# A fused two-layer attention and expert kernel: one attention bias as a unit of the shared experts, another bias moved to ScalarE

## The chip, the core and the metric

The kernel runs on one core of one Trainium2 chip. The metric is device time in microseconds (us), the median of several executions. Engines are named as in the profile: PE is TensorE (matmuls; PEld its weight loads), DVE is VectorE, ACT is ScalarE, POOL is GpSimd, SP is SyncE. Matmuls write to banks of 512 fp32 columns in PSUM; everything else of this kernel lies in SBUF or in device memory.

## The reference, cut to what matters

32 sequences of 256 tokens with 128 features (8192 tokens) go through two layers. Each layer is `x = x + attention(norm(x)) + experts(norm(x))`. Of the biases only two are touched:

```python
# layer 0: linear attention, 16 heads, and 8 routed experts (top 2) plus shared ones
out = einsum('bse,fe->bsf', out, Wo) + bo                     # bo: output bias
shared = silu(xf @ swg) * (xf @ swu) @ swd                    # 352 hidden units
# layer 1: causal attention, 8 heads, with a gate u
u = silu(x @ Wu.T + bu)                                       # bu: bias of units
out = (u * rms_norm(out, scale)) @ Wo.T + bo
```

All biases hold random values, so none can be left out.

## The kernel before, in words

The program is written out by hand for each engine; an engine runs its instructions in the order written, and semaphores are the only link between engines. Tokens are handled in 16 groups of 512 (four tiles of 128), `NG` = 16. Four stages follow one another:

1. **Attention 0** (about 0 to 255 us), steps 2 to 19. Step s works on group g = s - 2 (queries, keys and values, shared experts' hidden units) and on group e = s - 3 (its state, mixing and `output0`). Beside it LayerNorm, routing on DVE, and on POOL the sending of each routed row to its expert's region in device memory: 256 indirect DMAs, spread over the steps by the table `SENDS`, each behind a matmul of its step (`behind_attention0`). When all have landed, SP loads the first tile of rows of the experts; the last step's PE work (`rows_to_columns(0, 0, 3)`) waits for it, and `output0(15)` stands behind that on PE.
2. **Experts 0** (about 255 to 420 us): 36 tiles, bound by PE.
3. **Attention 1** (about 420 to 668 us), steps 2 to 20, same grouping: for group g keys, values and units, for group e = g - 1 energies and their use with the values, for y = g - 2 the output. DVE also adds the experts' rows of layer 0 (L1507), takes LayerNorm statistics and routes for layer 1.
4. **Experts 1** (about 668 to 936 us).

The lines that matter here:

- A product is exact to nearly fp32 by being split in high and low parts. A bias is likewise split in two rows (high and low) of the tile `bias` (`biases`, L1308 to L1311), and added by a matmul with ones: `bias_by_token` (L655) puts it along the tokens, `bias_by_feature` (L659) along the features. L655 is called in `keys_values0` (twice per group), in `output0` (once per group) and in attention 1's `v_of`; L659 in `u_of` alone.
- `output0(e)` adds into bank 7 the bias, then the attention's product (L748, 8 matmul instructions), then the shared experts' down product (L754, 24 instructions), whose hidden units `sh_h` come from DVE in three chunks of 128 (L1384). 352 units are used; the last 32 rows of the third chunk are zero padding.
- `constants_once` on DVE stands in the opening between LayerNorm statistics of groups 2 and 3 and before the split of the first weights (L1329) and columns (L1338), for which the first product of attention 0 (L674) waits.
- Attention 1, per group, around the change: PE `u_of` (bias L659, product L976, fp32 in four passes) into bank 1; ACT `tanh1` (L1888) of half the sum; DVE `units1` (L1561): (tanh + 1) * sum, read from bank 1. ACT then goes on with `keys_by_token` (L1894), `normalise` (L1673, rows of the LayerNorm, in the steps that have one), `heads1` (L1881) and `columns` (L1678). PE transposes these rows (L614), does the output (L1039, behind DVE's state L1565) and the next queries (L939). `keys_by_token` of PE (L981) also waits for the totals (ACT L1912) and, in steps with logits, for their copy (ACT L1691).
- POOL masks half of the energies with an affine select (L2109) that reads and writes SBUF, once per half step.

## Time and profile before

| | us |
|---|---|
| three runs | 933.10, 934.08, 941.79 |
| median | 934.08 |
| the profiled execution's own time | 937.29 |
| its span, first to last instruction | 935.8 |
| PE busy | 845.9 (90%) |
| DVE busy | 694.5 (74%) |
| ACT busy | 575.4 (61%) |
| POOL busy | 627.7 (67%) |

The mean granted TensorE clock is 0.975 of full. The busy shares are means over four stages with different limits: PE is 90% busy in the whole, yet in the attention stages it shares the chain of waits with DVE, ACT and POOL. So a change inside one stage is to be read in that stage: in the chain of waits there, and in the order of time around the line.

### The profile page before, as it was taken

Reading aid. Unit: us, or ns where it says so; the run is one execution under the profiler, and the core shown is the slowest. Engines: PE = TensorE matmul, PEld = TensorE weight load, DVE = VectorE, ACT = ScalarE, POOL = GpSimd, SP = SyncE. Lnnn points to the kernel's source line nnn. Section 1 sums busy time; section 2 is a strip of 40 time slices with the busy share of each in tenths; the row PEclk is TensorE's granted clock in tenths of the full one; section 3 lists DMA queues with packets and bytes.
Section 4 is the critical chain, followed back from the end, with each engine's and each line's share of the span. In section 5 each row is a group of like instructions: output and inputs, shape, how many; then the busy total and the mean of one; then the engine's idle time right before and its main releaser. Section 6 shows DMA issues by size and latency. Waiting matters only on the chain.

```text
span 935.8 us, 22379 instructions
## 1 busy us (share of the span) xinstructions
PE 845.9 (90%) x7975; PEld 752.8 (80%) x7975; DVE 694.5 (74%) x1809; ACT 575.4 (61%) x1185; POOL 627.7 (67%) x607
## 2 busy tenths in 40 slices
PE   3789999999699999997898888887899899999997
PEld 3678888889699998984566666665798899999996
DVE  7777787886377998885788788878654465668776
ACT  5756555454366777668886776654565375756652
POOL 4157677777105888876788788866777777666663
PEclk9999999999899999998999999989899899999999
DMA  9799992117449998951111111113776687789996
GB/s 269 233 407 397 395 385 67 48 52 236 166 144 286 311 302 263 289 163 54 37 39 41 35 36 43 42 34 112 278 237 200 214 283 258 255 296 344 363 365 184
DMA packets 130990, 191.06 MB, mean 204 GB/s; under 512 B 15808, under 2 KB 85952, under 8 KB 130752
## 3 DMA queue, kind: packets, MB, share of 16 engines
q1 hardware_dynamic: 96720, 141.21, 44.8%
q0 software_dynamic: 16640, 34.37, 11.1%
q10 hardware_dynamic: 17520, 14.06, 4.8%
q8 instruction: 64, 1.05, 0.5%
q14 instruction: 46, 0.38, 0.1%
HBM read 110.74 MB, written 80.97 MB: 205 GB/s over the span
## 4 chain that ended last, share of the span: by engine, by line
PE 58%; DVE 22%; issue 6%; ACT 5%; SPq 4%; DMA 3%; POOL 3%; DVEq 0%; POOLq 0%; ACTq 0%
PE pair L887 13%; PE pair L834 5%; PE pair L835 5%; PE pair L833 5%; PE pair L864 3%; PE pair L754 3%; PE pair L667 3%; PE pair L1031 2%; DVE a_en L1574 2%; PE pair L1008 2%; DVE X L1507 2%; ACT a_rows L1673 2%; DVE stats_t L1142 2%; PE pair L674 2%; PE pair L676 1%
## 5 line engine op out<-in xcount | busy, mean ns | idle before, releaser
L1992 POOL DMA_INDIRECT sent<-a_rows,slot x224 | 221.2, 987 | 84.3 <-issue 55.5
L2094 POOL DMA_INDIRECT back<-ex_tile_out,address x136 | 150.2, 1105 | 60.4 <-issue 31.1
L2003 POOL DMA_INDIRECT ex_joined<-outs,slot x128 | 132.1, 1032 | 86.6 <-DMA outs<-ex_tile_out 50.3
L833 PE MATMUL pair<-ex_x_hi,ex_w_hi 128*128 128x256 f32 x497 | 148.0, 298 | 0.0
L834 PE MATMUL pair<-ex_x_lo,ex_w_hi 128*128 128x256 f32 x497 | 142.1, 286 | 0.0
L835 PE MATMUL pair<-ex_x_hi,ex_w_lo 128*128 128x256 f32 x497 | 142.0, 286 | 0.0
L887 PE MATMUL pair<-ex_stage,ex_hid 128*128 128x128 f32 x1136 | 132.5, 275 | 0.0
L887 PEld LDWEIGHTS pair<-ex_stage,ex_hid 128*128 128x128 f32 x1136 | 130.0, 192 | 0.0
L1708 ACT ACTIVATE ex_w_hi<-ex_stage 128x768 fp32r<-128x768 f32 (+1 forms) x72 | 67.5, 937 | 91.6 <-DMA ex_stage<-in_experts 91.5
L1834 ACT ACTIVATE ex_hid<-pair,ex_stage 128x256 f32<-128x256 f32 x284 | 107.1, 497 | 0.1
L1345 DVE TENSOR_TENSOR ex_w_lo<-ex_stage,ex_w_hi 128x768 fp32r<-128x768 f32 (+1 forms) x72 | 77.4, 1075 | 31.6 <-ACT ex_w_hi L1708 30.8
L834 PEld LDWEIGHTS pair<-ex_x_lo,ex_w_hi 128*128 128x128 f32 x497 | 96.3, 194 | 0.0
L835 PEld LDWEIGHTS pair<-ex_x_hi,ex_w_lo 128*128 128x128 f32 x497 | 96.1, 193 | 0.0
L833 PEld LDWEIGHTS pair<-ex_x_hi,ex_w_hi 128*128 128x128 f32 x497 | 96.1, 193 | 0.0
L1986 POOL TENSOR_TENSOR rstd<-variance,minus_half 128x4 f32<-128x4 f32 x32 | 41.0, 1281 | 49.0 <-DVE variance L1147 48.5
L864 PE MATMUL pair<-ex_stage,ex_hid 128*128 128x128 f32 x568 | 69.7, 276 | 2.0 <-DVE ex_hid L1464 2.0
L864 PEld LDWEIGHTS pair<-ex_stage,ex_hid 128*128 128x128 f32 x568 | 66.5, 192 | 3.3 <-issue 3.2
L1673 ACT ACTIVATE a_rows<-X,shift,rstd 128x128 f32<-128x128 f32 x112 | 45.7, 486 | 30.2 <-DVE shift L1152 30.2
L1351 DVE TENSOR_TENSOR ex_x_lo<-pair,ex_x_hi 128x512 fp32r<-128x512 f32 x72 | 49.0, 680 | 15.3 <-ACT ex_x_hi L1714 14.6
L1824 ACT ACTIVATE ex_gate_s<-pair 128x512 f32<-128x512 f32 (+1 forms) x72 | 42.1, 587 | 27.4 <-PE pair L835 22.1
L674 PE MATMUL pair<-a_xT_hi,a_w_hi 128*128 128x512 f32 x112 | 49.5, 442 | 6.2 <-DVE a_xT_lo L1338 5.3
L1464 DVE TENSOR_TENSOR ex_hid<-ex_gate_s,pair 128x512 f32<-128x512 f32 (+1 forms) x72 | 48.9, 679 | 7.8 <-ACT ex_gate_s L1824 5.7
(247 smaller groups left out, 1992.7 us busy)
## 6 DMA issues: line engine op xcount, KB each, us to landing
ex_stage<-in_experts SPq DMA_DIRECT2D x72, 578.0 KB, 5.3
outs<-v_heads SPq DMA_DIRECT2D x8, 4352.0 KB
ex_stage<-in_experts SPq DMA_DIRECT2D x72, 320.0 KB, 4.2
ex_tile_in<-sent SPq DMA_DIRECT2D x72, 128.0 KB
outs<-ex_tile_out SPq DMA_DIRECT2D x71, 128.0 KB
ex_joined<-back ACTq DMA_DIRECT2D x15, 512.0 KB, 8.1
ex_tile_in<-sent SPq DMA_DIRECT2D x54, 132.0 KB
X<-in_x SPq DMA_DIRECT2D x16, 256.0 KB, 5.2
```

Source lines behind the costliest of these rows:

```text
L674: pe.matmul(o, w0_hi[:, c:c + P], hi, start=True, stop=False)
L833: pe.matmul(o[:, of_half], wh, x_hi[i % 2][:, of_half], start=True, stop=False)
L834: pe.matmul(o[:, of_half], wh, x_lo[i % 2][:, of_half], start=False, stop=False)
L835: m = pe.matmul(o[:, of_half], wl, x_hi[i % 2][:, of_half], start=False, stop=True)
L864: m = pe.matmul(bank[7][:, i * C:(i + 1) * C], hid[n % 2][c][:, i * P:(i + 1) * P], stage[0][n % NSTAGE[0]][:, i // HALF, 2 * F0P + c * C: ...
L887: m = pe.matmul(bank[b][:, s * C:(s + 1) * C], hid[n % 2][c][:, s * P:(s + 1) * P], stage[1][n % NSTAGE[1]][:, s // HALF, F1 + c * C:F1 + ...
L1345: dve.tensor_tensor(w_lo[layer][n % NSTAGE[layer]][:, 0:k, 0:u], stage[layer][n % NSTAGE[layer]][:, 0:k, 0:u], w_hi[i % 2][:, 0:k, 0:u].bi ...
L1708: act.activation(w_hi[i % 2][:, 0:k, 0:u], stage[layer][n % NSTAGE[layer]][:, 0:k, 0:u], ACT.Copy).then_inc(w_hi_here, 1)
L1834: m = act.activation(hid[n % 2][c][:, of_half], bank[c][:, of_half], ACT.Gelu, bias=stage[1][n % NSTAGE[1]][:, h, b1:b1 + 1])
L1992: pool.indirect_dma_start(out=sent[layer], out_offset=bass.IndirectOffsetOnAxis(ap=slot_i[layer][k][:, s, j:j + 1], axis=0), in_=rows[laye ...
L2003: pool.indirect_dma_start(out=joined[g % NJOIN][:, j, k, :], out_offset=None, in_=outs, in_offset=bass.IndirectOffsetOnAxis(ap=slot_i[0][k ...
L2094: pool.indirect_dma_start(out=back, out_offset=bass.IndirectOffsetOnAxis(ap=address[i % NSIDE][:, s // HALF, s % HALF:s % HALF + 1], axis= ...
```

## The change

Three things are edited.

- **bo of layer 0.** The matmul with ones in `output0` goes; the first product L748 starts the bank (`start=(i == 0)`). Row 96 of the third chunk of hidden units, until now padding, is set to 2.0 once by DVE, and the same row of the down weights (halved on the chip like the rest) holds bo. The second op of `shared_hidden` writes only the first 96 rows of the third chunk.
- **bu of layer 1.** The matmul L659 goes. `tanh1` gets half of bu as a per-partition bias. A new ACT instruction, `units1`, writes bank 1 plus bu to the SBUF tile `u1`, after ACT's `keys_by_token` and before `normalise`; it waits for results of layer 0 (at g = 1) and for `uo_ready`. DVE's `units1` takes its second operand from `u1` in SBUF and waits for `u1_here` too. PE's next users of bank 1 (`k_of`, the transposes) wait for `u1_here` in place of `u1_ready`.
- **Housekeeping.** `bias` has three blocks for five; `cols` has a fifth column; `constants_once` makes `half_bu` and four memsets; the loads of x of groups 8 to 15 share a semaphore by pairs.

```diff
@@ constants_once (DVE)
+                dve.tensor_scalar(half_bu[:], cols[:, 4:5], 0.5, None, ALU.mult)
+                for i in range(2):
+                    own(dve.memset(sh_h[i][2][SHARED_REST:P, :], 0.0))
+                    dve.memset(sh_h[i][2][SHARED_REST:SHARED_REST + 1, :], 2.0)
-                biases(0, 3 * C).then_inc(consts_made, 1)
+                biases(0, 2 * C).then_inc(consts_made, 1)
@@ next_layer_once (DVE)
-                biases(3 * C, 5 * C).then_inc(consts1_made, 1)
+                biases(2 * C, 3 * C).then_inc(consts1_made, 1)
@@ output0 (PE)
-                bias_by_token(7, 2 * C, C)
                 pe.wait_ge(mix0_ready, e + 1)
...
-                                  start=False, stop=False, skip_group_check=True)
+                                  start=(i == 0), stop=False, skip_group_check=True)
@@ shared_hidden (DVE)
+                k = SHARED_REST if c == 2 else P
-                dve.tensor_tensor(sh_h[g % 2][c][:], s, bank[3 + (2 * c + 1) % 3], ALU.mult).then_inc(sh_ready, 1)
+                dve.tensor_tensor(sh_h[g % 2][c][0:k, :], s[0:k, :], bank[3 + (2 * c + 1) % 3][0:k, :], ALU.mult).then_inc(sh_ready, 1)
@@ k_of, and the transposes of attention 1 (PE)
-                    pe.wait_ge(u1_ready, g)
+                    pe.wait_ge(u1_here, g)
@@ u_of (PE)
-                bias_by_feature(1, 4 * C)
-                pe.matmul(bank[1], w_attn1[:, 3 * C:4 * C], flat(xTg(g)), start=False, stop=True).then_inc(u1_done, 1)
+                pe.matmul(bank[1], w_attn1[:, 3 * C:4 * C], flat(xTg(g)), start=True, stop=True).then_inc(u1_done, 1)
@@ units1 (DVE)
                 dve.wait_ge(u1_tanh, g + 1)
-                if g == 1:
-                    results_back(dve, NTILES - 1)
-                dve.scalar_tensor_tensor(u1[g % 2][:], th1[1][:], 1.0, bank[1], ALU.add, ALU.mult).then_inc(u1_ready, 1)
+                dve.wait_ge(u1_here, g + 1)
+                dve.scalar_tensor_tensor(u1[g % 2][:], th1[1][:], 1.0, u1[g % 2][:], ALU.add, ALU.mult).then_inc(u1_ready, 1)
@@ ACT: a new function, and its place in the step
+            def units1(g):
+                act.wait_ge(u1_done, g + 1)
+                if g == 1:
+                    results_back(act, NTILES - 1)
+                if g >= 2:
+                    act.wait_ge(uo_ready, g - 1)
+                act.activation(u1[g % 2][:], bank[1], ACT.Identity, bias=cols[:, 4:5]).then_inc(u1_here, 1)
...
-                act.activation(th[:], bank[b], ACT.Tanh, scale=0.5).then_inc(said, 1)
+                act.activation(th[:], bank[b], ACT.Tanh, bias=bias, scale=0.5).then_inc(said, 1)
...
-                    tanh1(u1_done, g, 1, th1[1], u1_ready, u1_tanh)
+                    tanh1(u1_done, g, 1, th1[1], u1_ready, u1_tanh, half_bu[:])
                     keys_by_token(g)
+                    units1(g)
@@ host
+    swd[2 * P + SHARED_REST] = i["L0_attn_bo"]
```

## Rows read from the trace of the kernel before

**Rows 1.** The page, chain that ended last: share of the span by engine.

```profile
PE 58%; DVE 22%; issue 6%; ACT 5%; SPq 4%; DMA 3%; POOL 3%; DVEq 0%; POOLq 0%; ACTq 0%
```

**Rows 2.** Chain of waits, attention 0: start us, us, what.

```profile
64.50 0.24 PE pair L655
...
197.68 0.24 PE pair L655
```

**Rows 3.** Order of time on POOL: start, us, engine, line, op, tiles [idle before].

```profile
203.35 0.96 POOL L1992 DMA_INDIRECT sent<-a_rows,slot  x1 [0.72 <-PE pair L676]
204.73 0.96 POOL L1992 DMA_INDIRECT sent<-a_rows,slot  x1 [0.42 <-PE pair L676]
...
237.85 0.96 POOL L1992 DMA_INDIRECT sent<-a_rows,slot  x1 [0.31 <-issue]
```

**Rows 4.** Chain of waits, end of attention 0.

```profile
237.85 3.67 DMA sent<-a_rows,slot
...
246.78 0.43 PE pair L655
```

**Rows 5.** Order of time, all engines, opening.

```profile
1.20 0.22 DVE L1298 MEMSET scan<- 128x192 f32 x1
...
1.94 0.57 DVE L1303 MEMSET before<- 128x272 f32 x2
...
16.56 0.77 PE L674 MATMUL pair<-a_xT_hi,a_w_hi 128*128 128x512 f32 x1 [3.79 <-DVE a_xT_lo L1338]
```

**Rows 6.** Order of time, all engines, one step of attention 1.

```profile
483.17 0.48 PE L659 MATMUL pair<-ones_r,bias 128*128 128x512 f32 x1
...
484.08 0.21 ACT L1691 ACTIVATE logit<-pair 128x32 f32<-128x32 f32 x1
...
484.36 0.20 PEld L981 LDWEIGHTS pair<-consts,a_k 128*128 128x128 f32 x2 [0.68 <-ACT rms L1912]
...
484.55 0.60 ACT L1888 ACTIVATE a_th<-pair 128x512 f32<-128x512 f32 x1 [0.25 <-PE pair L976]
485.04 0.38 ACT L1894 ACTIVATE a_ktok<-pair 128x256 f32<-128x256 f32 x1
485.17 0.69 DVE L1561 SCALAR_TENSOR_TENSOR a_u<-a_th,pair 128x512 f32<-128x512 f32 x1 [0.78 <-ACT a_th L1888]
...
486.94 0.42 DVE L1565 TENSOR_TENSOR a_kv<-pair,consts 128x256 f32<-128x256 f32 x1 [1.07 <-PE pair L988]
```

**Rows 7.** Chain of waits, attention 1: steps where ACT or DVE decides.

```profile
427.15 3.07 ACT a_rows L1673 x8
...
561.68 0.59 DVE a_u L1561
```

**Rows 8.** Instructions on tile bias: duration ns min/median/max, first and last start, forms.

```profile
L1308 DVE CAST bias<-a_bias_raw x2: 294/320/345, 10.6 to 223.6; 128x384 fp32r<-128x384 f32 x1, 128x256 fp32r<-128x256 f32 x1
L1309 DVE TENSOR_TENSOR a_bias_raw<-a_bias_raw,bias x2: 427/493/559, 11.0 to 224.0; 128x384 f32<-128x384 f32 x1, 128x256 f32<-128x256 f32 x1
L1311 DVE SCALAR_TENSOR_TENSOR bias<-bias,consts,a_bias_raw x2: 485/552/618, 12.0 to 224.9; 128x384 fp32r<-128x384 f32 x1, 128x256 fp32r<-128x256 f32 x1
```

**Rows 9.** Order of time on ACT: instructions with a bias per partition.

```profile
486.84 1.51 ACT L1881 ACTIVATE a_kh<-a_k,consts 128x512 f32<-128x512 f32 x2
...
489.51 0.69 ACT L1814 ACTIVATE a_e<-pair,bqk1neg 128x512 f32<-128x512 f32 x1 [0.67 <-PE pair L939]
```

**Rows 10.** Order of time, DVE and POOL, three places in attention 1.

```profile
487.28 2.47 DVE L1507 SCALAR_TENSOR_TENSOR X<-ex_joined,gates_tok,X 128x128 f32<-128x128 f32 x8
...
500.54 1.10 POOL L2109 TENSOR_SCALAR_AFFINE_SELECT a_en<-a_en 128x1024 f32<-128x1024 f32 x1
500.57 3.32 DVE L1507 SCALAR_TENSOR_TENSOR X<-ex_joined,gates_tok,X 128x128 f32<-128x128 f32 x8
...
561.30 1.10 POOL L2109 TENSOR_SCALAR_AFFINE_SELECT a_en<-a_en 128x1024 f32<-128x1024 f32 x1
```

**Rows 11.** Stretch: length, busy us (instructions) of each engine, clock, DMA share, GB/s.

```profile
428.00:441.50 13.50, 10.17 (x104) 6.50 (x105) 8.15 (x25) 10.07 (x19) 8.87 (x9) 0.75 0.11 36
```

More of the change, by code:

```diff
@@ L52 @@
 SPLIT0 = 3 * C + 2 * FSP
+SHARED_REST = 352 - 2 * P
 WO0, SD0 = SPLIT0, SPLIT0 + C
@@ L249, in build @@
         gates = sb("gates", [P, 2, NARROW])
-        cols = sb("cols", [P, 4])
+        cols = sb("cols", [P, 5])
+        half_bu = sb("half_bu", [P, 1])
         bo1 = sb("bo1", [P, C])
@@ L258, in build @@
         bqk1neg = sb("bqk1neg", [P, 2])
-        bias = sb("bias", [P, 5 * C], F32R)
+        bias = sb("bias", [P, 3 * C], F32R)
         ones_r = sb("ones_r", [P, 512], F32R)
@@ L338, in build @@
         pads = a0("pads", [P, E, HALF, ROW])
-        bias_raw = a0("bias_raw", [P, 5 * C])
+        bias_raw = a0("bias_raw", [P, 3 * C])
         pad_addresses = a0("pad_addresses", [P, NPAD, HALF])
@@ L401, in build @@
         bank = [pair[i // 2][:, 512 * (i % 2):512 * (i % 2 + 1)] for i in range(8)]
-        x_dma = [sem(f"x_dma{g}") for g in range(NG)]
+        x_dma = [sem(f"x_dma{g}") for g in range(8 + (NG - 8) // 2)]
+        x_sem, x_count = [*range(8), *(8 + g // 2 for g in range(NG - 8))], [16] * 8 + [32] * (NG - 8)
         const_dma, small_dma, out_dma = sem("const_dma"), sem("small_dma"), sem("out_dma")
@@ L656, in bias_by_token @@
                           start=True, stop=False, skip_group_check=True)
-            def bias_by_feature(b, a):
-                pe.matmul(bank[b], bias[:, a:a + C], ones_r[:], start=True, stop=False)
             def rows_to_columns(layer, n, b):
@@ L967, in v_of @@
                 pe.wait_ge(q1_max, g + 1)
-                bias_by_token(0, 3 * C, C)
+                bias_by_token(0, 2 * C, C)
                 for i in range(GT):
@@ L1096, in tensor_program @@
                 for k, n in enumerate(COLUMNS[1].get(step, ())):
-                    pe.wait_ge(u1_ready, g + 1)
+                    pe.wait_ge(u1_here, g + 1)
                     if k == 1:
@@ L1137, in statistics @@
                 if layer == 0:
-                    dve.wait_ge(x_dma[g], 16)
+                    dve.wait_ge(x_dma[x_sem[g]], x_count[g])
                 else:
@@ L1882, in heads1, with tanh1 @@
                 m.then_inc(kh1_ready, 1)
-            def tanh1(done, g, b, th, ready, said):
+            def units1(g):
[5 more added lines that the diff above has]
+                act.activation(u1[g % 2][:], bank[1], ACT.Identity, bias=cols[:, 4:5]).then_inc(u1_here, 1)
+            def tanh1(done, g, b, th, ready, said, bias=0.0):
                 act.wait_ge(done, g + 1)
@@ L2189 @@
     swd = padded_rows(i["L0_ffn_swd"], 3 * P)
-    bias = np.concatenate([i[f"L0_attn_b{n}"] for n in "kvo"] + [i[f"L1_attn_b{n}"] for n in "vu"])[None, :]
+    swd[2 * P + SHARED_REST] = i["L0_attn_bo"]
+    bias = np.concatenate([i["L0_attn_bk"], i["L0_attn_bv"], i["L1_attn_bv"]])[None, :]
     arrays = {
```

6 lines of the change are left out of this document (3 added, 3 removed).

## The prediction

> **What bounds the kernel now.** I read the page's chain of waits first, then the chain in order of time through the two attention stages, then the order of time of each engine around the edited lines, and last the stretches with their granted clock. The page's chain is 58% PE, but 22% DVE and 5% ACT [rows 1], so a matmul that goes is worth something only where PE ends last. The experts' stages (some 430 us) hold nothing that is edited; they only start earlier or later.
>
> In attention 0 the chain runs through PE from the third bias matmul of a step on (L655 before L748 and L754) in seven steps up to 198 us; the first and the last of them stand in [rows 2], at 0.24 us each. In the others, among them the one from 178 to 193 us, it runs through ACT and DVE. From 203 us on POOL decides: its sends follow each other every 1.26 us (0.96 and a gap of 0.30) from 204.73 to 237.85 without a longer gap [rows 3]; they last waited for PE at 203.35 and 204.73, with gaps of 0.72 and 0.42. Then the last send lands, a tile is loaded, and PE does the last `output0` on the chain, bias at 0.43 us because the clock is at half [rows 4].
>
> In the opening, DVE ends last: the first product stands 3.79 us idle until DVE's split of columns [rows 5], and `constants_once` lies in DVE's queue ahead of it.
>
> In attention 1 a step takes 12 to 17 us. Steps are named here by their group g. PE's L659 is followed by L976 and L981. L981's weights are loaded at 484.36, straight after ACT's copy of the logits (484.08 + 0.21), not after L976 [rows 6]. DVE waits 0.78 us for the tanh before L1561, and 1.07 us for PE before L1565. The chain passes through ACT's normalised rows in g = 0 (427.15) and g = 1, and through DVE's L1561 in g = 3, 9, 10, 11, 13 and 14, of which the one of g = 9 stands in [rows 7].
>
> **The opening.** Four memsets of 512 columns are added. The nearest rows are 0.22 us for 192 columns and 0.57 for two of 272 [rows 5]: 0.285 each, or 0.065 more for 80 columns, which gives 0.22 + 320 x 0.0008 = 0.48 for 512. Four are 1.9 us, less a small overlap: 1.75. `half_bu` is one small instruction, 0.1. The biases shrink from 384 to 256 columns, which the two forms show directly: 0.05 + 0.13 + 0.13 us [rows 8], and about 0.1 for L1310 between them, 0.4 in all. Net 1.4 us, all of it on the path: DVE has no gap there. Bounds: 0.3 (memsets as short as the 0.22 row, 4 x 0.22 - 0.4 - 0.2 of overlap) and 2.1 (0.57 each, nothing of it overlapped). I take +1.4, by the slope. `biases` for layer 1 also shrinks, at 224 us, where POOL decides: nothing. Loads of x by pairs: groups 8 and 9 are first used 48 us in, when the loads have long landed: nothing.
>
> **Attention 0.** 16 matmuls go. Seven of them at 0.235 are on the chain before POOL takes over: 1.65 us. POOL can follow: it had 0.42 + 0.12 us of slack at 203.35 and 204.73 beyond its 0.30 gap [rows 3], and only one or two steps' savings (0.235 each) have to come out of it, as it waits for PE at the start of nearly every step before. The savings behind 203 us are lost, because the 27 sends left take 34 us whatever PE does. The last bias, 0.43 us at half clock [rows 4], is on the chain again. Together -2.1 us; bounds 0.43 (POOL keeps its times) and 16 x 0.235 + 0.2 = 4.0. DVE's op with 96 for 128 rows costs the same, as its length is set by columns. The down product has no more instructions than before.
>
> **Attention 1, the matmul.** L659 costs PE 0.24 us between starts, 16 times. But L981 cannot follow it: it is held by ACT's logits or totals [rows 6], which hang on the energies before L659. In g = 2 to 14 that leaves at most 0.03 us a step, 0.15 in all. Only in g = 15, without such a wait, the whole 0.24 comes through.
>
> **Attention 1, the new ACT instruction.** With a bias per partition an ACT op of 512 columns from PSUM takes 0.69 us (L1814) against 0.60 without (L1888) [rows 6, 9]. What counts is the distance between starts: 0.49 from L1888 to L1894 [rows 6], and 0.75 for each of the pair L1881 with two such operands [rows 9]; for one I take the middle, 0.62. So tanh + 0.13, copy + 0.62, and, where the tanh was waiting for PE, 0.24 earlier: `normalise` starts 0.51 later. In g = 0 the tanh waits for ACT itself, so 0.75. These two steps have ACT's rows on the chain [rows 7]: +1.26 us. In g = 2 to 8 the rows and so L614, L1039, L939 come 0.5 later too, but DVE is the one that ends the step there, with about 1 us to spare between the last use of values and DVE's gated units; nothing, and if that cover were gone, 0.5 each. Queued behind the copy on ACT are the rows, heads and columns; behind them PE's transposes.
>
> **Attention 1, DVE.** L1561 now waits for the copy: 0.35 + 0.38 = 0.73 us later than before where it waited for the tanh. In most steps the 1.07 us before L1565 [rows 6] take that up. Not in g = 10, where routing follows directly; it is counted below.
>
> There is a second cost, in the operands. Before, L1561 read one SBUF tile and PSUM; now it reads two SBUF tiles. Eight DVE ops with several SBUF inputs take 2.47 us beside DMA work of POOL, and 3.32 when they start inside an affine select (L2109): the DVE is held until the select has ended [rows 10]. L1561 itself started inside such selects in 11 of 16 steps, unhurt. From now on it would be held until about 0.54 us after the select's end (0.69 less the 0.15 of fixed time already spent). At g = 9 the select runs from 561.30 to 562.40 and L1561 started at 561.60 [rows 7, 10]: end at 562.94 for 562.28, +0.66, straight on the chain. By the same working g = 11 loses 0.6, g = 10 0.6 (with the wait above; its scan was being held already), g = 3 0.3 (PE was late there too), g = 13 and 14 under 0.05, and in g = 1, 2, 8 and 12 it ends before L1565 is due. Sum +2.2 us; bounds 0 and 16 x 0.6.
>
> The Trainium skill says of this, in "SBUF — State Buffer", section "Who interferes with whom", that a VectorE instruction with two SBUF inputs contends with a GpSimd instruction that reads SBUF, and that the one that starts first blocks the other. The trace agrees for the select (2.47 against 3.32), and by the page alone one would also fear the 7 steps in which VectorE comes first and the select is held for 0.69 us; the trace has no chain through the select there.
>
> **Sum.** 1.4 - 2.1 - 0.4 + 1.3 + 2.2 = +2.4 us. Against the profiled execution's own time of 937.29 that is 939.7. That execution lies 3.2 above the median of the three runs, 934.08; carried over, 936.5.
>
> **Rivals.**
>
> *PE is the bound wherever it loses a matmul* (faster). Then 32 matmuls at 0.235 go, 7.5 us, and the copies hide in ACT's idle time (39% of the span): 934.1 - 7.5 - 0.2 + 1.4 = 927.8. For it: PE at 90%. Against it: L981's wait, POOL from 203 us on. Chance 0.10.
>
> *The gains as forecast, the additions hidden* (about equal or a little faster). DVE's two-input op is not held because semaphores move it past the select, and the opening's memsets overlap: -2.1 - 0.4 + 0.3 + 0.5 = -1.7, 932.4. Chance 0.22.
>
> *The copy sits in every step* (slower). Place: ACT between `keys_by_token` and `normalise`, or `heads1` in steps without rows, with the transposes and the next queries behind it. It decides if the time from the rows to DVE's gated units shrinks by more than about 1 us in a step. Price: 16 x 0.62 = 9.9 for 1.3 + 2.2, so 934.1 + 1.4 - 2.1 - 0.4 + 9.9 = 942.9. For it: g = 0 and 1 are bound so now. Against it: DVE is without a gap before its gated units in g = 2 and 4 to 8. Chance 0.10.
>
> *The clock* (slower). In 428 to 441.5 the granted clock is 0.75 of full on average [rows 11], after PE had waited for ACT's rows; there half of the stretch ran at 1.2 GHz. A longer wait for rows could bring such a stretch to other steps. Price: 13.5 us with half of it at half speed lost about 3 us against its neighbours. Two more of them would give 936.5 + 6 = 942.5. Chance 0.06.
>
> *The matmuls go but time doesn't follow at all*, since the moved bias rides in products that run anyway: this is not in doubt, the instruction counts are plain.
>
> **Numbers.** The forecast has 0.52. Its own range is 934 to 939.5. The predicted time is 936.5. The range for 8 in 10 goes to the hidden-additions case and its lower bound of attention 0, 930.5, and up to just under the two slow rivals, 942. A measurement of this kernel tells about 1% (9.3 us) from no change: faster by more would need under 924.7, which no case reaches by its own sum (0.03, for the runs' own spread of 8 us); slower by more needs above 943.4, the upper edge of the two slow rivals (0.06).
>
> **What would show it.** First product at 18.0 in place of 16.56. No gap over 0.31 on POOL from about 204 on, and its last send some 0.2 us earlier than 237.85 (opening against savings). The gap before L981's weights still ended by ACT. `normalise` of g = 0 and 1 later by 0.75 and 0.5 behind the tanh. L1561 taking 1.0 to 1.5 us where it starts inside L2109. The attention 1 stage 3.1 us longer, and both experts' stages the same. It would be wrong if L1561 keeps 0.69 us in every step, if the first product keeps its 16.6, or if the span of attention 1 changes by over 5 us.

## The result, and the profile after

| | median us | runs | ratio to before |
|---|---|---|---|
| before, beside the change | 937.69 (933.10 to 943.92) | 15 | 1 |
| changed | 943.79 (938.65 to 950.05) | 15 | 1.0058 [1.0037, 1.0079] |
| before, in the third set of runs | 1033.25 | 35 | 1 |
| changed, in the third set of runs | 1036.07 | 12 | 1.0026 [0.9995, 1.0058] |

In the third set the kernel before too takes 1033 us, in another condition of the chip, and only the ratio is to be compared. The ratio on record, with its 95% interval, is not the quotient of the two medians: that is 1.0065 in the first measurement, or 6.1 us. By the ratios the change makes the kernel slower: 5.4 us (3.5 to 7.4) in the first measurement, 2.7 (-0.5 to 6.0) in the second, whose interval includes no change. The forecast was +2.4 and 936.5 us, in a range from 930.5 to 942.0. The direction held; the size and the range did not. Half of the 7.3 us from 936.5 to 943.79 is the kernel before itself: its 15 runs (the first three among them) have a median of 937.69, 3.6 above the 934.08 of the three to which the forecast was carried over. The rest, 5.4 us by the ratio against 2.4, is the subject here.

The profiled execution of the changed kernel took 938.86 us, span 937.4, against a span of 935.8 before. So the two traces differ by 1.6 us, not by 5.4: the profiled execution is the second fastest of the changed kernel's 15. What the traces show is therefore read stage by stage, against the spread that a stage has where nothing was edited.

The page of the changed kernel, first the busy time, then the chain that ended last:

```profile
PE 838.7 (89%) x7943; PEld 743.2 (79%) x7943; DVE 698.6 (75%) x1814; ACT 586.5 (63%) x1201; POOL 635.2 (68%) x607
...
PE 51%; DVE 23%; issue 7%; ACT 5%; POOL 5%; SPq 5%; DMA 3%; DVEq 0%; ACTq 0%; POOLq 0%
```

PE has 32 instructions fewer and is 7.2 us less busy, yet its share of the chain fell from 58 to 51% and POOL's rose from 3 to 5 [rows 1]. The chain moved to other engines by far more than 7.2 us. Part of this is a near tie that fell the other way: before, the chain goes through PE until 231.5 us, although POOL's gaps are no longer than 0.31 us from 204.73 us on [rows 3], and in the changed kernel it goes through POOL's sends from 206 us on. So the shares of the chain are no prices.

**Opening.** In order of time, the changed kernel on DVE and PE:

```profile
11.16 0.48 DVE L1326 MEMSET a_sh_h<- 32x512 f32 x1
11.81 0.48 DVE L1327 MEMSET a_sh_h<- 1x512 f32 x1 [0.17 <-DVE a_sh_h L1326]
12.35 0.48 DVE L1326 MEMSET a_sh_h<- 32x512 f32 x1
13.00 0.48 DVE L1327 MEMSET a_sh_h<- 1x512 f32 x1 [0.17 <-DVE a_sh_h L1326]
13.50 0.29 DVE L1307 CAST bias<-a_bias_raw 128x256 fp32r<-128x256 f32 x1
...
19.09 0.77 PE L675 MATMUL pair<-a_xT_hi,a_w_hi 128*128 128x512 f32 x1 [6.03 <-DVE a_xT_lo L1343]
```

Each memset has the 0.48 us of the estimate, but they occupy DVE from 11.16 to 13.50, 2.34 us: the second of a pair must wait for the first (0.17), and starts of independent ones are 0.54 apart (11.81 to 12.35), which is more than 0.48. PE's idle time before the first product grows from 3.79 [rows 5] to 6.03, and the product starts 2.53 us later. The rows of DVE account for all of it: 2.34 for the memsets, 0.28 from the start of `half_bu` to that of the first memset, less 0.38 for the shorter biases (1.58 us in place of 1.96), is 2.24; the other 0.29 are the landing of the first input, for which DVE waits until 5.72 us in place of 5.43 and which no edit touches.

**Attention 0.** On POOL, and then the chain of waits at the end of the stage:

```profile
204.68 0.96 POOL L2008 DMA_INDIRECT sent<-a_rows,slot  x1 [0.46 <-PE pair L677]
206.06 0.96 POOL L2008 DMA_INDIRECT sent<-a_rows,slot  x1 [0.42 <-PE pair L677]
...
239.40 0.95 POOL L2008 DMA_INDIRECT sent<-a_rows,slot  x1 [0.31 <-issue]
```

```profile
239.40 2.92 DMA sent<-a_rows,slot
...
246.51 1.09 PE pair L668 x4
247.60 1.71 PE pair L748 x8
249.31 2.96 PE pair L754 x24
```

As in [rows 3], POOL waits for PE up to 206 us and then runs at its own pace. DVE's first operation on the queries of a group stands 2.92 us later than before in g = 1, 2.40 in g = 7, 1.56 in g = 11 and 1.33 in g = 13; POOL's last send is 1.54 later. So of the 2.53 us of the opening 1.0 was won back before POOL decided; g = 14 and 15 fall to 1.06 and 0.79, which reaches nobody. On the last chain the products L748 follow the columns L668 without a bias between them [rows 4]. Experts 0 begins at 252.45 for 252.27: 2.53 lost, 2.35 won, at the first product of the experts.

**Attention 1.** The step of g = 9, in order of time, all engines:

```profile
562.88 0.17 ACT L1927 ACTIVATE rms<-pair 128x4 f32<-128x4 f32 x1
...
563.16 0.69 ACT L1903 ACTIVATE a_th<-pair,half_bu 128x512 f32<-128x512 f32 x1
563.20 0.20 PEld L980 LDWEIGHTS pair<-consts,a_k 128*128 128x128 f32 x2 [0.91 <-ACT rms L1927]
...
563.74 0.38 ACT L1909 ACTIVATE a_ktok<-pair 128x256 f32<-128x256 f32 x1
564.01 0.69 ACT L1897 ACTIVATE a_u<-pair,cols 128x512 f32<-128x512 f32 x1
...
564.50 1.10 POOL L2125 TENSOR_SCALAR_AFFINE_SELECT a_en<-a_en 128x1024 f32<-128x1024 f32 x1
564.58 1.64 ACT L1679 ACTIVATE a_rows<-X,shift,rstd 128x128 f32<-128x128 f32 x4
564.80 1.35 DVE L1567 SCALAR_TENSOR_TENSOR a_u<-a_th,a_u 128x512 f32<-128x512 f32 x1
...
565.56 1.48 POOL L2130 TENSOR_TENSOR rms<-rms,plus_half 128x4 f32<-128x4 f32 x1
```

The same step before, DVE's units and POOL's next instruction:

```profile
561.60 0.68 DVE L1561 SCALAR_TENSOR_TENSOR a_u<-a_th,pair 128x512 f32<-128x512 f32 x1
...
562.37 1.08 POOL L2114 TENSOR_TENSOR rms<-rms,plus_half 128x4 f32<-128x4 f32 x1
```

Line L980 (L981 before) has the same wait as in [rows 6], 0.91 for 0.68 us, ended by ACT (0.68 in g = 9 before, too): the matmul that went only lengthened the wait. DVE's units operation starts inside the affine select and takes 1.35 us in place of 0.69; it ends at 566.15, 0.55 after the select. POOL pays as well: its small TENSOR_TENSOR behind the select starts while DVE's held operation runs and takes 1.48 us for 1.08, ending 0.90 after DVE's. This is so in 10 of the 16 steps (1.48 to 1.53 us, for at most 1.16 before), and POOL is busy 635.2 us for 627.7. The forecast has no such term, and no run here shows what it costs in time. All 16 of DVE's operations by form, and the step of g = 4 in order of time:

```profile
L1897 ACT ACTIVATE a_u<-pair,cols x16: 688/690/692, 426.9 to 651.5; 128x512 f32<-128x512 f32 x16
L1567 DVE SCALAR_TENSOR_TENSOR a_u<-a_th,a_u x16: 691/700/2096, 427.7 to 652.3; 128x512 f32<-128x512 f32 x16
```

```profile
489.66 2.10 DVE L1567 SCALAR_TENSOR_TENSOR a_u<-a_th,a_u 128x512 f32<-128x512 f32 x1 [1.57 <-ACT a_u L1897]
490.10 1.10 POOL L2125 TENSOR_SCALAR_AFFINE_SELECT a_en<-a_en 128x1024 f32<-128x1024 f32 x1
```

Here DVE's row starts first, by 0.44 us, and DVE was held all the same, until 0.56 us after the select's end; the select kept its 1.10. The traces with the bu part alone and with the memsets at the top show the same step with 2.12 and 2.11 us. The Trainium skill says in "SBUF — State Buffer", section "Who interferes with whom", that the order of issue decides which of the two blocks the other. By the starts of the rows that did not hold in this step; but a row doesn't show when its instruction was issued, so the rule is neither confirmed nor refuted here. In g = 0 and 1 ACT's copy and rows are on the chain, and then the clock is low. Chain of waits of the changed kernel, answering to [rows 7]:

```profile
427.04 0.58 ACT a_u L1897
427.62 3.06 ACT a_rows L1679 x8
...
443.55 0.58 ACT a_u L1897
444.12 3.07 ACT a_rows L1679 x8
```

Two stretches of the changed kernel, g = 0 and g = 1, and the same two steps before (length, busy us and instructions of PE, PEld, DVE, ACT and POOL, granted clock, DMA share, GB/s):

```profile
421.90:436.70 14.80, 10.58 (x29) 5.66 (x29) 7.04 (x24) 10.85 (x22) 9.22 (x10) 0.57 0.14 47
436.70:454.30 17.60, 14.32 (x179) 9.50 (x179) 10.36 (x28) 13.28 (x25) 9.45 (x10) 0.79 0.09 28
```

```profile
422.80:436.20 13.40, 8.30 (x30) 4.44 (x30) 7.07 (x24) 10.23 (x22) 9.38 (x10) 0.80 0.16 52
436.20:451.80 15.60, 12.73 (x181) 8.95 (x180) 10.37 (x27) 12.60 (x24) 9.41 (x10) 0.96 0.10 32
```

The clock granted in g = 0 is 0.57 for 0.80 and in g = 1 0.79 for 0.96. That the change of this stage did it is not shown: the kernel with the bo part alone, whose attention 1 is the kernel before's, has clocks nearly as low and steps as long (14.4 and 17.5 us from query to query):

```profile
425.00:440.00 15.00, 10.07 (x34) 5.23 (x38) 7.57 (x24) 10.44 (x23) 8.75 (x9) 0.69 0.15 49
440.00:457.00 17.00, 14.12 (x179) 9.66 (x179) 9.92 (x28) 12.42 (x24) 9.48 (x10) 0.80 0.08 26
```

What a low clock costs stands in PE's products behind the rows of g = 1, first changed, then before:

```profile
449.71 2.04 PE L939 MATMUL pair<-xT,w_attn 128*128 128x512 f32 x2 [1.63 <-ACT xT L1684]
451.68 1.94 PE L1030 MATMUL pair<-a_en,v_heads 128*32 128x128 f32 x32
```

```profile
449.05 1.10 PE L939 MATMUL pair<-xT,w_attn 128*128 128x512 f32 x2 [1.74 <-ACT xT L1678]
450.07 1.08 PE L1031 MATMUL pair<-a_en,v_heads 128*32 128x128 f32 x32
```

The wait before them is as long as before (1.63 and 1.74), and the same instructions take 0.9 us more each at the lower of the two levels, 1.2 GHz.

### The profile page after: what moved, and what is told of

Its sections match the earlier page's. It is cut to its first block, busy times and chain, and to the rows that moved or that the text cites. A ratio compares the mean times of both kernels' runs of the same rounds, so it can differ in the third digit from the quotient of the medians.

```text
span 937.4 us, 22382 instructions
## 1 busy us (share of the span) xinstructions
PE 838.7 (89%) x7943; PEld 743.2 (79%) x7943; DVE 698.6 (75%) x1814; ACT 586.5 (63%) x1201; POOL 635.2 (68%) x607
## 4 chain that ended last, share of the span: by engine, by line
PE 51%; DVE 23%; issue 7%; ACT 5%; POOL 5%; SPq 5%; DMA 3%; DVEq 0%; ACTq 0%; POOLq 0%
PE pair L887 12%; PE pair L833 4%; PE pair L834 4%; PE pair L835 4%; POOL sent L2008 3%; PE pair L864 3%; PE pair L754 2%; PE pair L668 2%; DVE a_en L1580 2%; PE pair L1030 2%; PE pair L1007 2%; ACT a_rows L1679 2%; DVE stats_t L1141 2%; DVE X L1514 2%; SPq L558 2%
## 5 line engine op out<-in xcount | busy, mean ns | idle before, releaser
L2019 POOL DMA_INDIRECT ex_joined<-outs,slot x128 | 134.4, 1050 | 83.7 <-PE pair L668 47.4
L2110 POOL DMA_INDIRECT back<-ex_tile_out,address x136 | 152.2, 1119 | 55.9 <-issue 31.1
L833 PE MATMUL pair<-ex_x_hi,ex_w_hi 128*128 128x256 f32 x497 | 146.4, 295 | 0.0
L833 PEld LDWEIGHTS pair<-ex_x_hi,ex_w_hi 128*128 128x128 f32 x497 | 94.8, 191 | 0.0
L2002 POOL TENSOR_TENSOR rstd<-variance,minus_half 128x4 f32<-128x4 f32 x32 | 39.1, 1222 | 51.0 <-DVE variance L1146 50.6
L1486 DVE TENSOR_TENSOR ex_tile_out<-pair,ex_b2o 128x512 f32<-128x512 f32 (+1 forms) x37 | 24.8, 670 | 44.1 <-PE pair L887 43.8
```

What stands on the lines that cost most here:

```text
L833: pe.matmul(o[:, of_half], wh, x_hi[i % 2][:, of_half], start=True, stop=False)
L2019: pool.indirect_dma_start(out=joined[g % NJOIN][:, j, k, :], out_offset=None, in_=outs, in_offset=bass.IndirectOffsetOnAxis(ap=slot_i[0][k ...
L2110: pool.indirect_dma_start(out=back, out_offset=bass.IndirectOffsetOnAxis(ap=address[i % NSIDE][:, s // HALF, s % HALF:s % HALF + 1], axis= ...
```

## The experiments

Twelve measurements of eleven kernels, in three sets; a set shares a chip and 35 runs of the kernel before, and each of the twelve has 12 runs. In the second and third set the kernel before takes 1033 us. The instructions last nearly as long as elsewhere (L833 has a mean of 295 to 298 ns in the changed kernel), but its chain shows 5% of "another core or an unknown queue", some 50 of the 95 us, and DVE stands idle for 23 to 24 us somewhere between 738 and 772 us in all eight traces of this condition and in none of the first. The first set, at 938 us, and the second, at 1033, name the same chip. No run here tells what the cause is. So ratios and stages are compared only within one condition.

| kernel | ratio | interval |
|---|---|---|
| set 1: bo part alone | 1.0004 | 0.9976 to 1.0031 |
| bu part alone | 1.0027 | 1.0001 to 1.0053 |
| bo part, memsets at the top | 0.9982 | 0.9959 to 1.0005 |
| whole change, memsets at the top | 1.0021 | 0.9987 to 1.0055 |
| set 2: copy stays in PSUM | 1.0013 | 0.9992 to 1.0034 |
| no copy | 0.9992 | 0.9978 to 1.0006 |
| whole change, more matmuls in g = 0, 1 | 1.0006 | 0.9986 to 1.0026 |
| bo part at the top, more matmuls in g = 0, 1 | 0.9966 | 0.9939 to 0.9993 |
| set 3: whole change | 1.0026 | 0.9995 to 1.0058 |
| whole change, more matmuls in g = 0, 1 | 1.0001 | 0.9973 to 1.0028 |
| before, more matmuls in g = 0, 1 | 0.9989 | 0.9960 to 1.0018 |
| before without the 32 matmuls | 0.9981 | 0.9950 to 1.0013 |

The stages of the profiled executions, in us, worked out from the starts of these events: the first product, POOL's last send of attention 0, the first product of each expert stage, and DVE's first operation on the queries in g = 0 and g = 2 of attention 1; the last stage ends with DVE's last instruction.

| kernel | first product | to last send | to experts 0 | experts 0 | att. 1, g = 0, 1 | att. 1, rest | experts 1 |
|---|---|---|---|---|---|---|---|
| before | 16.56 | 221.3 | 14.4 | 170.6 | 29.0 | 217.5 | 264.1 |
| changed | 19.09 | 220.3 | 13.1 | 169.4 | 32.4 | 218.4 | 262.3 |
| bo alone | 18.77 | 220.1 | 13.6 | 172.6 | 31.9 | 215.8 | 265.0 |
| bu alone | 17.00 | 221.2 | 14.8 | 171.6 | 30.2 | 218.7 | 263.9 |
| bo, top | 16.19 | 220.1 | 13.4 | 173.1 | 30.0 | 217.4 | 264.5 |
| changed, top | 16.55 | 219.6 | 14.6 | 171.0 | 32.4 | 218.3 | 262.9 |
| *before, more matmuls* | 16.46 | 245.1 | 13.8 | 190.5 | 30.2 | 236.6 | 291.8 |
| *without the 32* | 16.45 | 243.0 | 12.9 | 191.1 | 31.4 | 236.2 | 295.1 |
| *changed, again* | 18.79 | 245.0 | 12.6 | 191.0 | 33.1 | 237.4 | 293.2 |
| *copy in PSUM* | 18.81 | 245.3 | 12.5 | 191.8 | 32.8 | 236.5 | 291.1 |
| *no copy* | 18.68 | 243.9 | 12.6 | 193.9 | 30.6 | 234.5 | 296.8 |
| *changed, more m.* | 18.67 | 243.7 | 12.4 | 189.1 | 30.2 | 238.1 | 293.7 |
| *changed, more m., again* | 18.97 | 244.7 | 13.5 | 190.9 | 30.2 | 238.3 | 295.5 |
| *bo, top, more m.* | 16.16 | 243.5 | 13.0 | 191.2 | 29.0 | 235.3 | 294.8 |

(In italics the second condition.) The expert stages carry none of the edits, and vary by 3.7 and 2.6 us in the first condition alone. A single trace can't be trusted for a sum; the attention stages are averaged over several kernels with the same part. The ratios have the same weakness: by its medians (937.18 against 937.79) the whole change with the memsets at the top would be 0.6 us faster than before, by its ratio 2.0 slower.

**The bo part alone, and with its memsets at the top.** Output bias as a unit, second attention as before:

```diff
 # bo alone: as in the change, bu's matmul, tanh and units as before
 # memsets at the top: the same four as the first instructions of DVE
+            for i in range(2):
+                own(dve.memset(sh_h[i][2][SHARED_REST:P, :], 0.0))
+                dve.memset(sh_h[i][2][SHARED_REST:SHARED_REST + 1, :], 2.0)
             dve.memset(ones_bf[:], 1.0)
```

> The kernel before with the part of layer 0 alone: bo as a unit of the shared experts, with the memsets where the change has them. Theory A (the cost is additive and lies in two places: 2.5 us in the opening, 4 to 5 us in attention 1, less 1.7 to 2.2 us in attention 0): the first product starts at about 19.1 us, attention 0 wins 1.7 us of that back before POOL takes over, the experts of layer 0 start within 0.4 us of before, attention 1 keeps its steps; in all 0 to +0.5 us against before. Theory B (PE is the bound and the matmuls were worth 0.235 us each): attention 0 wins 3.8 us, in all -1.3 us. Theory C (the loss is this part's, by the opening carried to the end): +2.5 us or more.

> The part of layer 0 alone, but its four memsets stand first in DVE's program, where DVE waits about 3 us for the first x. Theory A: the first product starts at 16.1 to 16.6 us (the biases are shorter by 0.4), attention 0 wins 1.7 to 2.2 us and nothing gives it back: -2.0 to -2.6 us against before, faster than before by 0.2 to 0.3%. Theory B: -4.2 us. Theory C': POOL's sends from 203 us on decide alone and keep their times: 0.

The opening in order of time, memsets at the top:

```profile
0.97 0.48 DVE L1297 MEMSET a_sh_h<- 32x512 f32 x1 [0.97 <-PEq L2211]
1.62 0.48 DVE L1298 MEMSET a_sh_h<- 1x512 f32 x1 [0.17 <-DVE a_sh_h L1297]
2.17 0.48 DVE L1297 MEMSET a_sh_h<- 32x512 f32 x1
2.82 0.48 DVE L1298 MEMSET a_sh_h<- 1x512 f32 x1 [0.17 <-DVE a_sh_h L1297]
...
16.19 0.76 PE L675 MATMUL pair<-a_xT_hi,a_w_hi 128*128 128x512 f32 x1 [3.54 <-DVE a_xT_lo L1341]
```

The same memsets cost nothing where DVE waits for input anyway: the first product is at 16.19, earlier than before by the shorter biases. With the memsets in place it is at 18.77. The difference is 2.58 us, of which 0.14 are the landing of the first input (5.47 for 5.33), so the place costs about 2.4. It is carried on: the experts of layer 0 begin at 249.74 us with the memsets at the top, 252.44 with them in place and 252.27 before. The ratios point the same way (1.0004 in place, 0.9982 at the top), but their intervals overlap and each includes 1. By the ratio the bo part without its opening is worth -1.7 us (-3.8 to +0.5); attention 0 was forecast at -2.1. Theory C of the part in place (+2.5 us) is at the edge of the ratio's interval (+2.9), and it is the trace that speaks against it.

**The bu part alone.** The change with the bo edits undone:

```diff
+                bias_by_token(7, 2 * C, C)
                 pe.wait_ge(mix0_ready, e + 1)
...
-                                  start=(i == 0), stop=False, skip_group_check=True)
+                                  start=False, stop=False, skip_group_check=True)
```

> The kernel before with the part of layer 1 alone: no matmul L659, the bias copy on ACT, the semaphores of x by pairs. Theory A: the opening and attention 0 as before; attention 1 from its first queries to the first tile of the experts after it 4 to 5 us longer: about 1.5 and 2 in g = 0 and 1, 0.6 to 1.0 in each of g = 3, 4, 9, 10, 11 where DVE's units op is held by POOL's select; in all +4 to +5 us. Theory B (PE bound): -3.8 us. Theory C (the loss is the opening's): 0.

Its ratio, 1.0027, is +2.5 us (+0.1 to +5.0); attention 1 is 248.9 us long for 246.5. That is near the prediction's terms for attention 1 (-0.4 + 1.3 + 2.2 = +3.1), and less than the 4 to 5 us expected for this run, which had been taken from the changed kernel's trace. Theory B (-3.8 us) is excluded.

**The whole change with the memsets at the top.** The edit is the one above, on the changed kernel.

> The whole change, the four memsets first in DVE's program. Theory A: 2.2 to 2.6 us less than the changed kernel, so +2.5 to +3.5 us against before; the first product at 16.2 to 16.8 us. Theory B and C: if the opening's loss is absorbed anyway, the same as the changed kernel.

1.0021 where the changed kernel has 1.0058: the first product comes 2.5 us earlier by the trace (16.55), and the ratios differ by 3.5 us with overlapping intervals. The expectation of +2.5 to +3.5 us against before was a little high for a ratio of +2.0.

**The copy left in PSUM.** Now DVE's units read one SBUF tile and PSUM, as before the change, while ACT does the same additional instruction:

```diff
-                act.activation(u1[g % 2][:], bank[1], ACT.Identity, bias=cols[:, 4:5]).then_inc(u1_here, 1)
+                act.activation(bank[1], bank[1], ACT.Identity, bias=cols[:, 4:5]).then_inc(u1_here, 1)
...
-                dve.scalar_tensor_tensor(u1[g % 2][:], th1[1][:], 1.0, u1[g % 2][:], ALU.add, ALU.mult).then_inc(u1_ready, 1)
+                dve.scalar_tensor_tensor(u1[g % 2][:], th1[1][:], 1.0, bank[1], ALU.add, ALU.mult).then_inc(u1_ready, 1)
```

PE's two users of bank 1 wait for `u1_ready` again.

> The whole change, but ACT's copy adds bu in place in PSUM bank 1; DVE's units op then reads one SBUF tile and PSUM as before, and PE waits for DVE's op before it reuses the bank. Theory A1 (DVE's op with two SBUF inputs is held by POOL's select, and that is half of the loss in attention 1): the op takes 0.69 us in all 16 steps, steps g = 3, 4, 9, 10, 11 are 0.5 to 1 us shorter than in the changed kernel, 2.5 to 3 us in all; g = 0 and 1 unchanged. Theory A2 (the copy's time on ACT is the whole loss): no step but those bound by ACT changes, and attention 1 stays at the changed kernel's length.

By form, and where the operation starts inside a select (g = 3):

```profile
L1567 DVE SCALAR_TENSOR_TENSOR a_u<-a_th,pair x16: 676/687/689, 474.8 to 711.2; 128x512 f32<-128x512 f32 x16
```

```profile
524.44 1.10 POOL L2125 TENSOR_SCALAR_AFFINE_SELECT a_en<-a_en 128x1024 f32<-128x1024 f32 x1
524.79 0.68 DVE L1567 SCALAR_TENSOR_TENSOR a_u<-a_th,pair 128x512 f32<-128x512 f32 x1
```

The longest of the 16 takes 0.69 us, though the operation stands as late as with the copy to SBUF and starts inside a select in 10 of the 16 steps. With the copy in SBUF it takes up to 1.31 us in this condition and 2.12 in the first. POOL's TENSOR_TENSOR behind the select is back at 1.04 to 1.07 us too. That settles what holds them: the second SBUF operand. In time it gives 1.3 us (1.0013 for 1.0026 in the third set), which the intervals can't tell from nothing; the rest of attention 1 is 236.5 us long for a mean of 237.9 of the three traces with the copy in SBUF. The 2.5 to 3 us that theory A1 expected were not found: the mechanism is shown, its price is not.

**No copy at all.** DVE reads bank 1 directly, bu only enters the tanh; this leaves the bias out of the linear factor of the units.

```diff
                     keys_by_token(g)
-                    units1(g)
...
-                dve.wait_ge(u1_here, g + 1)
```

> The whole change without ACT's copy: bu is left out of the linear factor of the units and stays only in the tanh; DVE reads bank 1 as before. Theory A: attention 1 within 1 us of the kernel before (only 0.1 us per tanh is left in g = 0 and 1), so 3.5 to 4.5 us less than the changed kernel, and in all +0 to +1 us against before (opening +2.5, attention 0 -2.3). Theory B (losing the matmuls shifts PE's clock stretches, the copy is harmless): attention 1 stays 3 us or more longer than before.

0.9992, 3.5 us less than the changed kernel (1.0026): the additional ACT instruction and the held operation together. The sum had 1.3 + 2.2 for the two. It is a difference of two sets with overlapping intervals, though, and the agreement may be partly luck: from g = 2 on this kernel's attention 1 is 234.5 us long, 1.7 to 2.1 shorter than in the two kernels of this condition whose DVE operation is the same as here (236.2 and 236.6).

**More matmuls in g = 0 and g = 1.** Four products of 512 columns in each of the two steps, into a bank that nobody reads, while PE waits for the rows: one ahead of the transposes, one behind the first set and two behind the second. The waits for the readers of that bank are left out below. They were put into the changed kernel, the kernel with the bo part at the top and, in the third set, the kernel before.

```diff
+                if warm:
+                    pe.matmul(bank[4], w_attn1[:, 0:C], flat(xTg(0)), start=True, stop=True)
                 for k, n in enumerate(COLUMNS[1].get(step, ())):
...
                     transposes(1, n, 1 - k)
+                    if warm:
+                        for _ in range(k + 1):
+                            pe.matmul(bank[4], w_attn1[:, 0:C], flat(xTg(0)), start=True, stop=True)
```

> The whole change, with four extra fp32 matmuls of 512 columns (into bank 4, which is free then; their result is not used) in each of g = 0 and 1, where PE waits for ACT's rows: one before the transposes, one after the first, two after the second. Theory D (a part of the loss in g = 0 and 1 is TensorE's clock, which falls to half when PE idles behind the later rows): no stretch at half clock between 428 and 457 us, and the two steps 2 to 3.5 us shorter together than in the changed kernel. Rival: the clock falls anyway or the steps hang on ACT alone: no gain, or a loss of up to 2 us by the extra matmuls.

> The part of layer 0 alone with the memsets first, and the same extra matmuls in g = 0 and 1 of attention 1. Theory D: 1.5 to 3 us less than without the extra matmuls, so -3.5 to -5 us against before, the fastest of all kernels here. Rival: the same as without them, -2 us.

> The changed kernel with four more matmuls of 512 columns that write a bank nobody reads, in PE's wait for ACT's normalised rows in g = 0 and g = 1 of attention 1. Theory (an additional stretch at half clock in these two steps costs 2 us of the change's price): 1.5 to 2.5 us less than after_again, and g = 0 at 14.2 us and g = 1 at 16.0 in place of 14.8 and 17.6. Rival (the price is DVE's held op and the later rows alone, and the clock moves nothing): equal to after_again within 0.7 us.

> The kernel before with the same four additional matmuls in g = 0 and g = 1 of attention 1, and nothing of the change. Theory (the clock in these steps also costs the kernel before something: 13.5 us at 0.75 of full clock on average): 0.5 to 2 us faster than before, ratio 0.998 to 0.9995. Rival (the clock stretches only move to a later place, so nothing is gained): ratio 0.9995 to 1.0005.

The two steps of the changed kernel without the additional matmuls, and with them (columns as above, second condition):

```profile
467.30:482.90 15.60, 10.60 (x33) 6.21 (x37) 6.98 (x23) 10.91 (x23) 8.02 (x9) 0.63 0.12 40
482.90:500.50 17.60, 13.33 (x179) 8.75 (x179) 10.48 (x28) 13.09 (x25) 9.52 (x10) 0.90 0.08 28
```

```profile
468.00:482.30 14.30, 12.72 (x57) 7.11 (x61) 7.00 (x23) 10.97 (x24) 8.71 (x9) 0.76 0.14 48
482.30:498.30 16.00, 14.72 (x179) 8.88 (x171) 10.69 (x28) 13.07 (x26) 9.52 (x10) 1.00 0.10 31
```

With more work on PE both steps are granted a higher clock (0.76 and 1.00 for 0.63 and 0.90), and are 3.0 us shorter. With the additional matmuls the changed kernel needs 30.2 us for them twice and the two kernels with the copy absent 30.2 and 29.0. Without them it is 33.1 (copy in PSUM 32.8) against 31.4 and 30.6 (the 32 matmuls left out; no copy). By these means ACT's copy is worth about 0.6 us in the two steps with the additional matmuls and 2.0 without them, but kernels with the same attention 1 differ by as much (30.2 and 29.0). The ratios move the same way, by 2.6 us in the changed kernel (1.0026 to 1.0001) and 1.1 in the kernel before, within their intervals. The rival that the low clock merely moves to a later place is borne out in part: from g = 2 on attention 1 is 238.1 and 238.3 us long with the additional matmuls and 237.4 without, at a mean granted clock of 0.95 and 0.94 for 0.96. Of the 2.9 us won in the two steps, 0.7 to 1.0 go again there, and attention 1 as a whole is 2.0 to 2.2 shorter.

The bo part at the top with these matmuls has the lowest ratio of all kernels, 0.9966, or -3.5 us (-6.3 to -0.7): the only one below its reference by more than its interval.

**The whole change once more, and the kernel before without its 32 matmuls.** The latter leaves out both biases and puts nothing in their place:

```diff
-                bias_by_token(7, 2 * C, C)
...
-                bias_by_feature(1, 4 * C)
-                pe.matmul(bank[1], w_attn1[:, 3 * C:4 * C], flat(xTg(g)), start=False, stop=True).then_inc(u1_done, 1)
+                pe.matmul(bank[1], w_attn1[:, 3 * C:4 * C], flat(xTg(g)), start=True, stop=True).then_inc(u1_done, 1)
```

> The changed kernel once more, as the measure for the other three of this set. Theory (a sum of three parts: opening +2.5 us, attention 0 -2.3, attention 1 +3 to +4.5): ratio to before 1.004 to 1.006. Rival (the 5 us of the first measurement were mostly where the clock happened to fall in attention 1, and do not come back): ratio 1.000 to 1.002.

> The kernel before without the two matmuls with ones in each step, and with nothing in their place: it leaves out the first attention's output bias and the second's bias of units. It shows what the 32 matmuls alone are worth. Theory (only where PE ends last: 2.1 us in attention 0, 0.4 in attention 1): ratio 0.997, the last send of POOL 0.5 to 2 us earlier than before, attention 1 equal within 0.5 us. Rival (PE bound everywhere): 32 x 0.235 = 7.5 us less, ratio 0.992.

What the 32 matmuls are worth is 2.0 us (0.9981; interval -5.2 to +1.3 us, so no gain is not excluded), and not 7.5. In the stages, against the kernel before with more matmuls: 2.1 up to POOL's last send, 1.0 from there to the experts, 0.4 in attention 1 from g = 2 on (236.2 for 236.6). The forecast had 2.1 for the first two together and 0.4 for the last; the 3.1 here lies inside its bounds, 0.43 to 4.0. It is no test of where POOL takes over, however. In this condition POOL still waits late in the stage: 1.29 us before its send at 254 us, for something not recorded, in the kernel without the matmuls, and 1.27 us before that at 256 us, for PE, in the other. In the first condition its gaps are 0.30 or 0.31 us from 206 us on. The repeated measurement of the change gave 1.0026, between the theory's 1.004 to 1.006 and the rival's 1.000 to 1.002. It excludes neither.

## Why the prediction was wrong in size and right in its mechanisms

| step | forecast us | measured us | from |
|---|---|---|---|
| opening | +1.4 | +2.2 | changed (2.24) and bo alone (2.21); the other 0.3 of the changed kernel's 2.53 are the first input's landing |
| attention 0 | -2.1 | -2.1 | means: -1.2 to the last send, -0.9 behind it |
| attention 1, g = 0, 1 | +1.3 | +1.4 | means; +3.4 in the changed kernel's own trace |
| attention 1, rest | +1.8 | +1.5 | means; 2.2 less 0.4 in the sum |
| sum | +2.4 | +3.0 | |
| base of the forecast | 934.08 | 937.69 | 3 runs; 15 runs |

The means are taken over the first condition: four traces with the bo part against two without; three with the bu part (31.7 and 218.4 us for the two parts of attention 1) against three without (30.3 and 216.9). The averaged lengths of attention 0 lie within 0.7 us up to the send and 1.5 behind it; those of g = 0 and 1 within 2.2 us with the bu part and 2.9 without, those of the rest within 0.4 and 1.7. With so few traces the +1.4 is not clear of chance.

- **Two steps failed, the base and the opening.** The step "carried over, 936.5" took the median of three runs for the kernel before; 15 runs gave 937.69, 3.6 us more, and the range had no room for it. In the sum the term mis-sized is the opening, +1.4 against 2.2. The forecast took 0.48 us a memset, which the trace shows to the digit, and "less a small overlap: 1.75". There is no overlap. `own` makes the second memset of a pair wait, 0.17 us each, and the starts are 0.54 apart even without a wait: 2.34 us, 0.6 more than the term. `half_bu` took 0.28 up to the first memset for 0.1, and the biases gave back 0.38 for 0.4. The edit shows `own` around two of the four, so the waits were there to be counted. The upper bound, 2.1, left them out too; by its own terms (4 x 0.57 + 0.1 - 0.4) it is 2.0.
- **Attention 0 was right** in where POOL takes over (206 us for 204), in the loss of all that is saved behind it, and in the bias at the end. The last send was expected 0.2 earlier and is 1.54 later: 1.4 - 1.65 was forecast, 2.53 - 1.0 is measured. That the whole is -2.1 to the digit is luck: the forecast had 1.65 before the send and 0.43 behind it, the means have 1.2 and 0.9.
- **L981 was right**: its weights start 5.45 us after DVE's first operation on the queries, in the kernel before and in the changed one alike, in g = 3, 5, 8 and 9. The kernel without the matmuls is 0.4 shorter there, which is no more than the spread of that stage.
- **ACT's copy was right in its delay**: the rows begin 0.67 us later behind the tanh's start in g = 0 and 0.66 in g = 1 (0.75 was expected in both, of which 0.24 comes back in g = 1 through the earlier tanh), and 0.43 later in the step in g = 3, 5, 8 and 9. The time that this costs in g = 0 and 1, 1.3 against 1.4, is no confirmation, since the clock moves the same two steps by more.
- **DVE's held operation was right in mechanism and partly in place.** 1.35, 1.31 and 1.19 us in g = 9, 3 and 11 against 0.66, 0.3 and 0.6 over the usual; 0.84 in g = 10, where the late start spent most of it. Missed were g = 6 (1.12), where DVE starts inside the select, and g = 4 (2.10), where its row starts first. The forecast feared a held select in seven steps where VectorE comes first. That count doesn't fit its own 11 of 16 inside a select: in the trace before, the select starts within DVE's operation in g = 10 alone. What is held after the change is DVE, and behind it POOL's TENSOR_TENSOR, not the select. The steps' lengths took part of it back: in the changed kernel's trace g = 2, 3 and 4 grew by 0.60, 0.63 and 0.99 and g = 9, 10 and 11 by 0.67, 0.42 and 0.60, but g = 5, 6, 7 and 13 became shorter by 0.43, 1.02, 0.12 and 1.21.
- **The clock was kept apart as a rival** with 6 us and a chance of 0.06, and the forecast's term for g = 0 and 1 leaves it out. These two steps show low clocks in most traces, and sorted by the other part of the change they differ more than by this one: 31.7 us on average in the four kernels with the bo part (30.0 to 32.4) against 29.6 in the two without (29.0 and 30.2), a difference of 2.1 in a stage that the bo part doesn't edit; from g = 2 on it is -0.6. The granted clock of g = 0 is 0.57 to 0.69 in those four and 0.75 and 0.80 in the two. Whether the bo part does this, by what it changes before, or chance, was not tested; the second condition has no trace of the kernel before as it is.
- **The other rivals fell.** PE as the bound everywhere (927.8, or -6.3 us) is excluded by the first measurement, by the bu part alone, and by the kernel without the matmuls. Hidden additions (932.4) are excluded by the first measurement, whose lower end is +3.5 us, and by the held rows. A copy in every step (942.9, +8.8 with its terms) would need attention 1 to be 9.5 us longer; it is 2.9, and 4.3 in the changed kernel's own trace.

What stays open: the stages sum to +3.0 us, the first measurement says +5.4 with a lower end of 3.5, the second +2.7. The two parts' own ratios add up to 1.0031, or +2.9. Some 2 us of the first number are in none of the rows of the table. Two things on record point at the clock. One is the 2.1 us by which g = 0 and 1 are longer in kernels with the bo part. The other is the mean granted clock of every run: 0.9715 over the 15 of the changed kernel, and 0.9718, 0.9730 and 0.9732 in the other kernels with the bo part, against 0.9753 with the bu part alone and 0.9745 over the first set's 35 runs of the kernel before. Among those 35 a run is 6.5 us longer for each 0.01 of clock that it lacks, so 0.003 is an estimated 2.0 us. This is a relation between runs and not an experiment, and in the second condition it is not seen (0.950 to 0.952 with the bo part and without). The range failed by 1.8 us mainly because its base was a median of three runs: a base 3.6 us off was larger than every term of the sum.

## What to carry to other kernels

A one-time initialisation is priced by its place: four memsets cost about 2.4 us behind the first input and nothing ahead of it, which is as much as the 2 us that attention 0 won. Before moving an operand of VectorE from PSUM to SBUF, look at what GpSimd does at that moment: each can hold the other up, and in one step VectorE was held even though its row starts first. And when the expected effect is 3 us of 935, carry it over to a median only with the spread of that median in the range, and read the sum over several traces, since a single one varies by more in stages that nobody touched.

## What the hardware showed that was not expected

- DVE with two SBUF operands was held by an affine select whose row starts 0.44 us after its own: 2.10 us for 0.69, in three traces of the same step. All held operations end 0.55 or 0.56 us behind the select's end, in all six traces with the copy in SBUF. With one operand in PSUM the longest of 16 took 0.69.
- POOL's small TENSOR_TENSOR that starts while such a DVE operation runs takes 1.48 to 1.55 us for 1.04 to 1.16, and ends 0.90 or 0.91 behind DVE's.
- A row's duration is not what it occupies: memsets of 512 columns have rows of 0.48 us and starts 0.54 apart, and 0.65 apart where one waits for the other. ACT's additional instruction has a row of 0.69 and takes 0.58 of the chain.
- Four needless matmuls in each of two steps raised their granted clock from 0.63 and 0.90 to 0.76 and 1.00 and made them 3.0 us shorter together; 0.7 to 1.0 of it was lost again in the steps behind, at a lower clock.
- The same kernel took 938 us in one condition and 1033 in another at nearly equal instruction durations, with waits for something that the trace doesn't record.
